# Short TensorE stages of a four-layer graph network take no wait of a later stage

## The reference

```python
# x: (128, 128, 256), adj: (128, 128, 128), all float32
x = ln(x + (adj @ (x @ W0 + b0)) / adj.sum(-1))                   # layer 0
q, k = split(x @ Wqk); w = scale * mask * (q * (adj @ (k * mask))).sum(-1)
x = ln(x + softmax(w)[:, :, None] * (x @ Wv))                     # layer 1
x = ln(x + attention(x, scores * (adj + adj), 8 heads) @ Wo + bo) # layer 2
H = adj != 0                                                      # layer 3, twice:
conv(h) = Dinv * (H @ (Binv * (H.T @ (h @ W.T)))) + b
x = ln(conv2(ln(relu(conv1(x)))) + x + x)
```

## Time and profile before

| | us |
|---|---|
| median of 3 runs | 1778.93 |
| range | 1777.81 to 1779.14 |
| the profiled execution | 1777.09 |
| its span, first to last instruction | 1775.3 |

### The profile page before, as it was taken

The page is one execution under the profiler, slowest core; times in us unless marked ns, Lnnn a source line. Parts: engine busy times, 40 slices in busy tenths (PEclk is TensorE's granted clock), DMA queues, the critical chain, the costliest instruction groups (busy, mean ns, idle before and its releaser), DMA issues. The chain is left out here.

```text
span 1775.3 us, 51999 instructions
## 1 busy us (share of the span) xinstructions
PE 1739.4 (98%) x15358; PEld 1564.2 (88%) x15358; DVE 1463.3 (82%) x4038; ACT 1454.2 (82%) x4463; POOL 1386.3 (78%) x2825
## 2 busy tenths in 40 slices
PE   7999999999999999999999999999999999999997
PEld 6888888889888898888898888988888988989886
DVE  7888888888888888888888888888888888888886
ACT  5888788888878887888888788878888887888786
POOL 4777778787788777787877887777878778777776
PEclk9999999999999999999999999999999999999999
DMA  4111101111001111011110011110111100111000
GB/s 130 31 43 42 33 18 32 41 41 37 20 25 41 41 41 33 16 34 41 41 36 21 27 41 41 41 32 17 34 41 41 33 23 27 41 41 41 27 6 22
DMA packets 93590, 62.94 MB, mean 35 GB/s; under 512 B 8430, under 2 KB 92924, under 8 KB 93564
## 3 DMA queue, kind: packets, MB, share of 16 engines
q1 hardware_dynamic: 92748, 61.58, 11.6%
q10 hardware_dynamic: 816, 1.05, 0.2%
HBM read 45.82 MB, written 16.78 MB: 35 GB/s over the span
## 5 line engine op out<-in xcount | busy, mean ns | idle before, releaser
L779 ACT ACTIVATE z<-z,z_max 128x128 f32<-128x128 f32 x1024 | 399.3, 397 | 5.4 <-DVE z_max L1119 3.9
L880 POOL TENSOR_TENSOR ln_rs<-ln_ve,minus_half 128x1 f32<-128x1 f32 x640 | 353.2, 552 | 50.0
L878 POOL TENSOR_TENSOR ln_ve<-ln_mv,eps_col 128x1 f32<-128x1 f32 x640 | 122.8, 192 | 178.7 <-DVE ln_mv L1025 175.8
L883 POOL TENSOR_SCALAR ln_nm<-ln_mv,ln_rs 128x1 f32<-128x1 f32 x640 | 171.2, 268 | 110.1 <-POOL ln_rs L880 109.9
L900 POOL TENSOR_TENSOR z<-z,z_rcp 128x1024 f32<-128x1024 f32 x128 | 243.0, 1899 | 8.7 <-DVE z_rcp L1126 5.5
L510 PE MATMUL ps<-w2T,mnT 128*128 128x256 f32 x1536 | 208.6, 284 | 0.0
L510 PE MATMUL ps<-w1T,txT 128*128 128x512 f32 x768 | 205.1, 404 | 0.1
L779 ACT ACTIVATION_READ_ACCUMULATOR z<-z,z_max 128x1 f32 x1024 | 198.2, 194 | 0.0
L510 PEld LDWEIGHTS ps<-w2T,mnT 128*128 128x128 f32 x1536 | 187.8, 188 | 4.2 <-DVE mnT L1035 0.4
L1035 DVE TENSOR_TENSOR mnT<-ps,mnT 128x512 fp32r<-128x512 f32 x128 | 86.8, 678 | 112.1 <-ACT mnT L710 112.0
L1119 DVE TENSOR_REDUCE z_max<-z 128x4 f32<-128x512 f32 x256 | 170.0, 675 | 0.1
(11 more groups left out here) (154 smaller groups left out, 4928.9 us busy)
## 6 DMA issues: line engine op xcount, KB each, us to landing
x_in<-in_x_dram SPq DMA_DIRECT2D x128, 128.0 KB, 2.1
a_hold<-in_adj_dram SPq DMA_DIRECT2D x128, 128.0 KB, 2.2
out_dram<-y_out SPq DMA_DIRECT2D x128, 128.0 KB, 1.7
a_in<-in_adj_dram SPq DMA_DIRECT2D x128, 64.0 KB, 1.9
h<-in_L_gnn_W_dram SPq DMA_DIRECT2D x2, 512.0 KB, 7.3
x<-in_L_gnn_Wqk_dram ACTq DMA_DIRECT2D x1, 512.0 KB, 3.6
y_out<-in_L_gnn_W_dram ACTq DMA_DIRECT2D x1, 256.0 KB, 4.4
y_out<-in_L_gnn_Wv_dram ACTq DMA_DIRECT2D x1, 256.0 KB, 5.3
```

What stands on the lines that cost most here:

```text
L779: m = act.activation(z[:, g % 2, h, :], z[:, g % 2, h, :], ACT.Exp, bias=z_max[:, g % 2, h:h + 1], accum_out=z_sum[:, g % 2, h:h + 1])
L878: pool.tensor_tensor(ve[n][:, g:g + 1], mv[n][:, g, 1:2], (eps4_col if n == "ln4" else eps_col)[:, :], ALU.add).then_inc(eps_made[n], 1)
L880: pool.tensor_tensor(rs[n][:, g:g + 1], ve[n][:, g:g + 1], minus_half[:, :], ALU.pow).then_inc(root_made[n], 1)
L883: pool.tensor_scalar(nm[n][:, g:g + 1], mv[n][:, g, 0:1], rs[n][:, g:g + 1], -1.0, ALU.mult, ALU.mult).then_inc(shift_made[n], 1)
```

## The change

The forced wait is gone: at, amx and mp issue only their own waits, so what they took for the next stage stands at that stage's head (or, where the next stage is the head of the next, ahead of its first pass). Also, early skips the wait on a bank whose last owner is the very stage that the next one reads (SOURCE names it: cx reads pt, wo reads cx, h0 reads ax and so on), because the stage itself waits for that reader anyway. The tables of orders and banks are the same.

```diff
+SOURCE = {"h0": "ax", "xg": "x1t", "v1": "x1t", "v2": "x2t", "cx": "pt", "wo": "cx", "h1": "tx", "y": "mn"}
...
                 for other, og, away in owners:
+                    if (other, og, away) == (SOURCE.get(stage), g, a):
+                        continue
                     later = ((s, 0 if s in per_group else og, away) for s in FOLLOWS.get(other, ()))
...
-            def room(left, free=False):
+            def room(left):
 
-                if left < group["passes"] and left <= group["slots"] or free:
+                if left < group["passes"] and left <= group["slots"]:
                     next(group["next"], None)
...
             def at(a, g, o):
-                room(1, True)
                 return pe.transpose(o[:, 0:P], a_in[:, g, :], ident[:, :])
...
             def amx_(a, g, o):
-                room(1, not need(norm_made["ln0"], a, g))
+                need(norm_made["ln0"], a, g)
...
             def mp_(a, g, o):
-                room(1, not need(hb_made, a))
+                need(hb_made, a)
```

## The result

The changed kernel takes 1754.3 us (median of 4 runs, 1754.08 to 1754.82), the kernel before 1778.4 us on the same chip (4 runs, 1777.76 to 1779.14). The ratio is 0.9865, with an interval of 0.9848 to 0.9882: 24.1 us less, where 15.5 were forecast. The profiled execution took 1754.82 us with a span of 1753.1, so the spans differ by 22.2 us (1775.3 before).

A forecast was written before the change was run, and what follows sets the result against it. TensorE, busy 98% of the span, was taken as the bound, so only its waits could change. Of 0.63 us a turn 0.50 pass wm; 31 x 0.50 = 15.5 us off gives 1763.4 us, range 1757 to 1771.

The forecast's parts named there:

- (a): At amx.2: it loses the wait on copy pT, cx.2 takes it and starts 0.63 us a turn sooner.
- Rival 2: Only part arrives, as cx.2's loads keep their 0.33 us gap or doubled waits cost: 0.30 us a turn, 1769.6 us; 20%.
- (b): Behind cx.2: x1t.3 holds with 0.04 us to spare; GpSimd's wm stays put and lets 0.50 us a turn through.
- (c): At mp: mp.3 takes mp.2's wait on z; the loop's jump holds cx.0, so 0, ends 0 and 0.31 us.
- (d): At the turn's head: at loses waits, v2.2, wo.0 and ax.1 gain some; 0 a wait, upper end 0.05 us.
- (e): Waits going back to h0.2, h0.3, cx.1, xg.0, wo.3: ScalarE's queue sets cx.2's time, so gain 0.
- (f): First and last group: first at.0 need not wait for x, no amx in the last; 0 each.
- Rival 1: wm moves or its bound is softer: 0.63 us a turn, 1759.4 us; with half the mp gain 1754.7; 15%.

The follow-up runs named there:

- amx_only: The kernel before, with one edit: amx issues no forced wait of the next stage; 1758.5 us, ratio 0.9891.
- before_xb: The kernel before, with GpSimd's xb.0 and xb.1 moved from ahead of wm into its idle time of the turn before; 1778.6 us.
- after_xb: The changed kernel, with GpSimd's xb.0 and xb.1 moved from ahead of wm into its idle time of the turn before; 1746.0 us.
- after_pad_last: The changed kernel plus a 4-column product on GpSimd right ahead of wm, its tile placed behind all others; 1761.3 us.
- mp_only: The kernel before, with one edit: mp issues no forced wait, so mp.3 takes mp.2's wait on z; 1772.4 us, ratio 0.9970.

## Why the prediction was right in kind and wrong in size

- **(a) amx.2 and cx.2: right.** 0.63 us forecast, 0.60 measured alone (amx_only). cx.2 starts 0.06 us behind the copy, as rows 5 had suggested. Rival 2's 0.30 us is out, but not because the gap of 0.33 us went: it stands behind amx.2 in every run, and since amx.2 now ends before the copy it lies under the copy. amx.2 with its gap takes 0.63 us, which doesn't quite fit into 0.56 us of idle time; the sum left that out.
- **(b) x1t.3: right.** No wait at it is listed after.
- **(b) wm as the bound: right place, mis-sized.** This is the term of the sum that failed. It was put at 0.50 us a turn and was 0.71. By itself that would not have taken the time below the range: had only (a) arrived, the 1758.5 us of amx_only would have been the result. It took the zeros of (c), (d) and (e) as well. The 0.50 from wm's end to wt's load are there to the hundredth. Left out were 0.11, the lead of a load over its product, and 0.10 by which wm itself comes sooner. "GpSimd does not move with TensorE" and "So wm stays where it is" were wrong by that: from GpSimd's wait to the second instruction of c3 it is 22.85 us before (941.72 - 918.87, its start is in the rows below) and 22.83 after, but from there to wm 2.43 and 2.36. Before, the last xg's result w reached wm 0.14 us ahead of its start, after 1.17 us ahead (the next two rows of w, of before and after). So before, wm waited for w, which TensorE's xg makes by way of VectorE. before_xb shows it (last rows): there c3 is ready 0.12 us sooner, wm starts 0.14 us behind w all the same, and from c3's second instruction to wm it is 2.54 us. In the eight kernels of this study where w comes 0.25 us or more ahead and nothing is added between, that is 2.34 to 2.37, however early w is. Of the 0.10 us, 0.07 are this; the other 0.03 are differences of 0.01 to 0.02 between single rows.

```profile
941.72 2.42 POOL L956 TENSOR_TENSOR c<-c,b_all 128x1024 f32<-128x1024 f32 x1
...
943.93 0.08 DVE L1058 DVE_READ_ACCUMULATOR2_ANT w<- 128x1 f32 x1
```

```profile
931.23 0.08 DVE L1064 DVE_READ_ACCUMULATOR2_ANT w<- 128x1 f32 x1
```

```profile
942.62 2.42 POOL L956 TENSOR_TENSOR c<-c,b_all 128x1024 f32<-128x1024 f32 x1
...
944.94 0.08 DVE L1059 DVE_READ_ACCUMULATOR2_ANT w<- 128x1 f32 x1
...
945.16 0.20 POOL L919 TENSOR_TENSOR wm<-w,mask 128x4 f32<-128x4 f32 x1
```

- **(c) mp: wrong.** 0 forecast, 0.19 measured alone, within the ends of 0 and 0.31 that were given. The sentence that failed is "something else holds it, and I take it to be the jump": a gap that stands behind an instruction moves with that instruction and hides nothing. The same gap of 0.12 us stands ahead of cx.1, where there is no jump, so that it is the jump's isn't shown either.
- **(d) at and doubled heads: nearly right.** 0.09 us a turn from at.2, which had been called free or bound anyway. Doubled waits cost nothing that can be seen. The Trainium skill, Perfetto Trace Analysis, section Identifying Dependency Chains, says that an instruction with waits on several engines may get separate semaphore instructions ahead of it; whether they are there or not, the distances at these heads are the same within 0.01 us.
- **(e) waits that go back to their own stage: wrong.** 0 forecast, 0.28 measured alone. It rested on "the trace lists no idle time there", and the waits of 0.12 to 0.16 us that ScalarE had were hidden by its overlapping records.
- **(f) first and last group: right.** The first at.0 doesn't wait for x any more; 22.0 of the 22.2 us are in the turns.
- **The chances.** The errors have one sign and then one lid: 0.56 us a turn too little was taken for (c), (d) and (e), and with (a) 1.16 us arrive, but since wm cuts them to 0.71, the turns are off by 31 x 0.21 = 6.5 us only. The time is 9.1 us below the forecast: the rest is 0.2 us outside the turns, 1.9 by which the profiled executions differ less than the medians, and 0.6 by which the median of before came out lower. That the miss isn't larger is luck: 1.16 us arrived where 0.63 were expected, and only the chain that was taken for the bound kept 0.45 of them from the time. "It matters little: what is gained here meets the same bound at wm" was right in principle, and it made the bound's size the one number on which the forecast hung. Rival 1 (wm moves, or its bound is softer), with half of (c), gave 1754.7; it came about, in part for its own reason. It was given 15%, and its 1754.7 was left outside the range, where it ought to have been in it: the bound rested on one difference of two rows, and the other terms all erred on the side of nothing.

## What to carry to other kernels

Where a wait moves from one engine to another, the gain is the lead of the next chain, and this lead is to be read on the instruction that carries the work (the product), not on one that runs ahead of it (its load). An engine whose records overlap is to be called free of waits only when the distances of the starts agree with those elsewhere, not when no idle time is listed. And a move on an engine off the path is to be tried again after each change of the path: the same move of two GpSimd instructions gave nothing before the change and 8.3 us behind it.

## What the runs showed that was not expected

**32 bytes.** Products that stream x2T in 512 columns went from 390 to 395 ns when the tile moved from byte 118144 to 118176 of each partition, and their loads from 227 to 234 ns apart: 24 x 7 = 168 ns a turn. The turn less what wm holds is 0.22 us longer (w1T's products, of 512 columns too, went from 403 to 405 ns), the turn itself 0.13. Why, and whether another place would be faster than the present one, wasn't tried. An added tile is thus not a neutral edit, and belongs behind all others in an experiment. All tiles behind the new one moved; of what these products read, x2T is the only one that did, since wqT and wkT stand ahead of it.

**The clock in the last group.** TensorE's granted clock stays at its upper level through the loop. In the last group it fell in some executions. From 1700 to 1720 us of after_xb, then from 1710 to 1720 us of the changed kernel (its next 10 us at 1.00 too) (span, busy us, granted clock, DMA):

```profile
1700.00:1710.00 10.00, 8.58 (x86) 0.85 0.11 39
1710.00:1720.00 10.00, 10.00 (x100) 0.81 0.01 2
```

```profile
1710.00:1720.00 10.00, 8.18 (x102) 1.00 0.11 38
```

The same stretch of work, with 1.4 and 1.8 us of idle time at its start, ran with a granted clock of 0.85 and 0.81 in the one, so in part at the lower level of 1.2 GHz, and at the upper level of 2.4 GHz throughout in the other. From the last wt to the end it took 71.6 us in after_xb, in after_pad_last and in the traced run of mp_only (71.7), and 70.1 in the changed kernel. mp_only shows it within one kernel: its five runs with a granted clock of 1.000 over the whole program took 1772.1 to 1772.6 us, its two with 0.997 took 1774.2 and 1774.3. Near 31 us, at the start of the program, the clock fell too in some traces (0.66 from 30 to 35 us of after_xb, 1.00 in the changed kernel). That is up to 2 us of a time and no property of the loop, and the reason why the turns tell these kernels apart better than the medians.
